# A fused attention and feed-forward layer on one core: first unit's attention moved beside the last-but-two projection, last output tile split in two column halves

## The reference

```python
def reference(x, w_qkv, b_qkv, w_out, b_out, gate_w, up_w, down_w, gate_s, up_s, down_s):
    h = layernorm(x)
    q, k, v = split(h @ w_qkv.T + b_qkv)              # 16 heads of 32
    # linear attention with decay, chunks of 128 tokens:
    #   out = (q * decay_q) @ S + ((q @ k.T) * dmask) @ v
    #   S   = lam_c * S + (k * decay_k).T @ v
    x = x + layernorm(attention(q, k, v) @ w_out.T + b_out)
    h = layernorm(x)
    g = silu((h @ fp8(gate_w)) * gate_s) * ((h @ fp8(up_w)) * up_s)
    return x + layernorm((g @ fp8(down_w)) * down_s)
```

## Time and profile before

| | us |
|---|---|
| median of 3 runs | 980.73 |
| profiled execution | 980.54 |
| its span, first to last instruction | 978.7 |
| TensorE busy | 949.6 (97%) |
| VectorE busy | 696.8 (71%) |
| GpSimd busy | 691.3 (71%) |
| ScalarE busy | 510.6 (52%) |
| mean granted clock of TensorE | 0.997 |

### The profile page before, as it was taken

The page is one execution under the profiler, slowest core; times in us unless marked ns, Lnnn a source line. Parts: engine busy times, 40 slices in busy tenths (PEclk is TensorE's granted clock), DMA queues, the critical chain, the costliest instruction groups (busy, mean ns, idle before and its releaser), DMA issues.

```text
span 978.7 us, 21882 instructions
## 1 busy us (share of the span) xinstructions
PE 949.6 (97%) x8412; PEld 700.8 (72%) x8412; DVE 696.8 (71%) x1357; ACT 510.6 (52%) x987; POOL 691.3 (71%) x839
## 2 busy tenths in 40 slices
PE   8999999999888999999999999999999999999996
PEld 7687777777666776867778776767767676776764
DVE  6999998985887775767567576766757676675422
ACT  5666555565655464636355463635546363544522
POOL 3799998887776585948567584856758495775633
PEclk9999999999999999999999999999999999999998
DMA  9798899989976673846658284665838475512100
GB/s 320 232 309 245 244 261 314 281 260 301 244 204 144 138 195 66 183 108 142 157 103 190 55 199 97 152 146 115 180 59 199 94 161 121 139 44 44 44 23 22
DMA packets 199354, 159.87 MB, mean 163 GB/s; under 512 B 141649, under 2 KB 141777, under 8 KB 199121
## 3 DMA queue, kind: packets, MB, share of 16 engines
q1 hardware_dynamic: 198384, 157.86, 65.3%
q10 hardware_dynamic: 864, 0.61, 0.2%
HBM read 82.93 MB, written 41.94 MB: 128 GB/s over the span
## 4 chain that ended last, share of the span: by engine, by line
PE 44%; DVE 18%; POOL 16%; issue 10%; DMA 4%; SPq 3%; ACT 3%; POOLq 0%; DVEq 0%; ACTq 0%
PE bank L919 18%; PE bank L937 17%; PE att L896 5%; DVE stats L1386 3%; POOL rstd L1053 3%; POOL att_pool L1118 3%; DMA dram_qk<-qk_hl 2%; POOL vv L1103 2%; DVE state_hl L1460 2%; POOL qk_hl L1083 2%; SPq L297 2%; DVE w_pool L1523 2%; POOL xr L1128 1%; POOL rstd L1050 1%; DVE state L1449 1%
## 5 line engine op out<-in xcount | busy, mean ns | idle before, releaser
L919 PE MATMUL bank<-f_pool,up_q 128*128 128x256 f16 x1536 | 183.7, 273 | 4.2 <-DVE w_pool L1523 2.8
L919 PE MATMUL bank<-f_pool,gate_q 128*128 128x256 f16 x1536 | 183.6, 273 | 4.1 <-ACT w_pool L617 3.9
L937 PE MATMUL bank<-down_q,w_pool 128*128 128x512 f16 x768 | 168.3, 379 | 0.0
L919 PEld LDWEIGHTS bank<-f_pool,up_q 128*128 128x128 f16 x1536 | 148.1, 98 | 26.8 <-DVE w_pool L1523 8.5
L919 PEld LDWEIGHTS bank<-f_pool,gate_q 128*128 128x128 f16 x1536 | 146.3, 98 | 26.9 <-ACT w_pool L617 6.5
L1118 POOL TENSOR_TENSOR att_pool<-p,att_pool 128x512 f16<-128x512 f32 x128 | 145.7, 1159 | 24.5 <-ACT att_pool L569 24.5
L1523 DVE SCALAR_TENSOR_TENSOR w_pool<-bank,us_t,w_pool 128x256 f32<-128x256 f32 x192 | 84.1, 480 | 109.9 <-ACT w_pool L617 54.7
L1050 POOL TENSOR_TENSOR rstd<-mv,eps_t 128x1 f32<-128x1 f32 (+1 forms) x113 | 32.4, 287 | 182.0 <-DVE mv L1392 181.8
L937 PEld LDWEIGHTS bank<-down_q,w_pool 128*128 128x128 f16 x768 | 74.1, 98 | 86.9
L1136 POOL TENSOR_TENSOR w_pool<-w_pool 128x512 f16<-128x512 f32 x96 | 111.2, 1164 | 29.3 <-ACT w_pool L623 29.2
L569 ACT CAST att_pool<-p 128x512 f16<-128x512 f32 x128 | 75.6, 619 | 53.7 <-DVE p L1430 53.0
(11 more groups left out here) (147 smaller groups left out, 1824.4 us busy)
## 6 DMA issues: line engine op xcount, KB each, us to landing
dram_qk<-qk_hl SPq DMA_DIRECT2D x64, 256.0 KB, 4.6
att_pool<-dram_qk SPq DMA_DIRECT2D x64, 256.0 KB, 6.0
f_pool<-dram_qk SPq DMA_DIRECT2D x64, 256.0 KB, 6.0
xr<-in_x SPq DMA_DIRECT2D x31, 512.0 KB, 4.6
dram_kd<-kd_hl SPq DMA_DIRECT2D x32, 256.0 KB, 2.8
dram_v<-vv SPq DMA_DIRECT2D x32, 256.0 KB, 4.4
qn_pool<-dram_qk SPq DMA_DIRECT2D x32, 256.0 KB, 9.1
out_x<-w_pool SPq DMA_DIRECT2D x32, 256.0 KB, 2.1
```

The source lines that it names most:

```text
L919: ins = nc.tensor.matmul(b[:, j * TOK:(j + 1) * TOK], w[:, k, o * P:(o + 1) * P], x1_hl[:, v % 2, part, k], start=(k == 0 and part == 0), ...
L937: ins = nc.tensor.matmul((b_gate, b_up)[t][:, :], h_hl[:, part, k, t * P:(t + 1) * P], down_q[:, k], start=(k == 0 and part == 0), stop=(k ...
```

## The change

- A new `last_ahead` replaces `ahead(13)` on TensorE, ScalarE, GpSimd and VectorE. It has the scores of unit 0's first chunk between qk(13,2) and v(13,0), and the state of that chunk between the v blocks. The v blocks of unit 13 go to `b_gate` and `b_up`, as `b_s` now holds scores.
- `first_slot` attends chunk 0 after qk(14,0), then works on chunk 1, whose `attend(0, 1)` and the first scores of unit 1 stand ahead of v(14,1).
- `second_slot` has qk(15,0) and qk(15,1) apart, both project blocks together, and qk(15,2) and qk(15,3) behind attend(1,0). The orders of ScalarE, GpSimd and VectorE change with it.
- On SP, spill_v(13) goes ahead of load_xr(0); turn_o_tile(0,0) and spill_kd(14) move up.
- In slot 17, y2_normalise(14, 0) stands behind silu(15, 0).
- Tile 1 of unit 15 is made in two halves of 256 columns in two banks (48 matmuls of 256 columns), scaled and summed by halves, centred on VectorE while GpSimd takes the root, finished by VectorE, and stored by two DMAs, one from ScalarE's queue and one from SP's.

```diff
         def v_bank(n, t):
-            return b_s[t][:, :] if n < LEAD else (b_gate, b_up)[t][:, :]
+            return b_s[t][:, :] if n < LEAD - 1 else (b_gate, b_up)[t][:, :]
...
+            spill_v(LEAD - 1)
             load_xr(0)
-            spill_v(LEAD - 1)
             spill_q(LEAD)
+            turn_o_tile(0, 0)
             sp.wait_ge(score_mm, 8)
             load_unit(2, 0)
             load_unit(2, 1)
-            turn_o_tile(0, 0)
             spill_k(LEAD)
             sp.wait_ge(state_mm, 2)
             load_unit(2, 3)
+            spill_kd(LEAD)
             turn_o_tile(0, 1)
-
-            spill_kd(LEAD)
             spill_v(LEAD)
...
-            store(units - 1, 1)
...
+            sp.wait_ge(last_d, 2)
+            sp.dma_start(last_tile[:, cols(1)], y2[:, 1, cols(1)]).then_inc(stored[1], 16)
...
             def second_slot():          # ScalarE
                 n = LEAD + 1
+                o_hi_tile(0, 1)
+                probs_hi(1, 0, 0)
                 q_hi(n, 0)
-                o_hi_tile(0, 1)
+                v_hi_tile(LEAD, 1)
+                probs_hi(1, 0, 1)
                 q_hi(n, 1)
-                probs_hi(1, 0, 0)
                 state_hi(1, 0)
                 y_normalise(0, 0)
-                probs_hi(1, 0, 1)
+                y_normalise(0, 1)
+                probs_hi(1, 1, 0)
+                x1_hi(0, 0)
                 k_hi(n, 2)
-                y_normalise(0, 1)
-                k_hi(n, 3)
-                x1_hi(0, 0)
-                probs_hi(1, 1, 0)
                 x1_hi(0, 1)
                 probs_hi(1, 1, 1)
                 state_hi(1, 1)
+                k_hi(n, 3)
...
                 silu(v, 0)
+                if v == units - 1:
+                    y2_normalise(v - 1, 0)
...
-                y2_normalise(v, 0)
-
+                if v != units - 2:
+                    y2_normalise(v, 0)
...
+            act.wait_ge(last_d, 1)
+            act.dma_start(last_tile[:, cols(0)], y2[:, 1, cols(0)]).then_inc(stored[1], 16)
...
+            def down_by_halves(v):
+                pe.wait_ge(h_d, 6 * v + 6)
+                for h, b in enumerate((b_up, b_gate)):
+                    if h:
+                        pe.wait_ge(y2_d, 2 * v + 1)
+                    for k in range(IT):
+                        for part in range(2):
+                            ins = nc.tensor.matmul(b[:, cols(h)], h_hl[:, part, k, P:TOK], down_q[:, k, cols(h)],
+                                                   start=(k == 0 and part == 0), stop=(k == IT - 1 and part == 1))
+                    ins.then_inc(down_mm, 1)
...
+            def last_ahead():           # TensorE
+                k = LEAD - 1
+                for i in range(3):
+                    project_qk(k, i)
+                scores(0, 0, 0)
+                project_qk(k, 3)
+                scores(0, 0, 1)
+                project_v(k, 0)
+                carry_and_state(0, 0)
+                project_v(k, 1)
+
             def first_slot():
-                scores(0, 0, 0)
-                carry_and_state(0, 0)
                 project_qk(LEAD, 0)
-                scores(0, 0, 1)
-                project_qk(LEAD, 1)
-                project_qk(LEAD, 2)
                 attend(0, 0)
                 scores(0, 1, 0)
+                project_qk(LEAD, 1)
+                scores(0, 1, 1)
+                carry_and_state(0, 1)
+                project_qk(LEAD, 2)
                 project_qk(LEAD, 3)
-                scores(0, 1, 1)
                 project_v(LEAD, 0)
-                carry_and_state(0, 1)
+                attend(0, 1)
+                scores(1, 0, 0)
                 project_v(LEAD, 1)
-                attend(0, 1)
 
             def second_slot():
                 n = LEAD + 1
-                scores(1, 0, 0)
                 project_qk(n, 0)
+                scores(1, 0, 1)
                 project_qk(n, 1)
                 carry_and_state(1, 0)
                 project(0, 0)
-                scores(1, 0, 1)
                 project(0, 1)
-                project_qk(n, 2)
-                project_qk(n, 3)
                 attend(1, 0)
                 scores(1, 1, 0)
-                project_v(n, 0)
+                project_qk(n, 2)
                 scores(1, 1, 1)
                 carry_and_state(1, 1)
+                project_qk(n, 3)
+                project_v(n, 0)
                 project_v(n, 1)
                 attend(1, 1)
...
+            def last_ahead():           # GpSimd
+                k = LEAD - 1
+                inverse_std_x(k + 2)
+                v_lo(k - 1)
+                state_decay(0, 0)
+                q_lo(k, 0)
+                q_lo(k, 1)
+                probs_lo(0, 0, 0)
+                x_lo(k + 2)
+                kd_lo_half(k, 0)
+                probs_lo(0, 0, 1)
+                kd_lo_half(k, 1)
+
             def first_slot():
-                state_decay(0, 0)
-                probs_lo(0, 0, 0)
-                probs_lo(0, 0, 1)
                 v_lo(LEAD - 1)
+                state_decay(0, 1)
                 q_lo(LEAD, 0)
+                probs_lo(0, 1, 0)
                 q_lo(LEAD, 1)
-                state_decay(0, 1)
-                probs_lo(0, 1, 0)
+                probs_lo(0, 1, 1)
                 kd_lo_half(LEAD, 0)
-                probs_lo(0, 1, 1)
                 kd_lo_half(LEAD, 1)
-                v_lo(LEAD)
 
             def second_slot():
                 n = LEAD + 1
                 state_decay(1, 0)
+                probs_lo(1, 0, 0)
+                v_lo(LEAD)
                 q_lo(n, 0)
-                probs_lo(1, 0, 0)
+                probs_lo(1, 0, 1)
+                inverse_std_of(LN_Y, 0, 0)
+                inverse_std_of(LN_Y, 0, 1)
+                residual(0, 0)
                 q_lo(n, 1)
-                inverse_std_of(LN_Y, 0, 0)
-                residual(0, 0)
-                probs_lo_block(1, 0, 2)
-                inverse_std_of(LN_Y, 0, 1)
-                probs_lo_block(1, 0, 3)
                 residual(0, 1)
                 inverse_std_of(LN_X1, 0, 0)
-                state_decay(1, 1)
+                probs_lo(1, 1, 0)
                 inverse_std_of(LN_X1, 0, 1)
                 x1_lo(0, 0)
-                probs_lo(1, 1, 0)
                 x1_lo(0, 1)
+                state_decay(1, 1)
                 probs_lo(1, 1, 1)
...
+            def last_part(h):
+                dve.wait_ge(down_mm, 2 * units + h)
+                nc.vector.tensor_tensor(y2[:, 1, cols(h)], (b_up, b_gate)[h][:, cols(h)], ds_t[:, cols(h)], ALU.mult).then_inc(y2_d, 1)
+                dve.wait_ge(y2_d, 2 * units + h)
+                nc.vector.bn_stats(stats[:, LN_Y, h], y2[:, 1, cols(h)]).then_inc(bn_d[LN_Y2], 1)
...
+            def last_ahead():           # VectorE
+                k = LEAD - 1
+                moments_x(k + 2)
+                scale_h()
+                k_lo(k, 2)
+                dve.wait_ge(tab_in, 16 * N_TAB)
+                dve.wait_ge(*x_landed(units - 2))
+                masked(0, 0, 0)
+                k_lo(k, 3)
+                masked(0, 0, 1)
+                v_sum(k, 0)
+                carry_and_state(0, 0)
+                v_sum(k, 1)
```

More of the change, by code:

```diff
@@ L257, in over_e, with cols @@
             return table.unsqueeze(2).to_broadcast([P, KT, DH])
+        last_tile = out_u[units - 1, T - 1]
+        def cols(h):
+            return slice(h * D // 2, (h + 1) * D // 2)
         def third(w, part, half):
@@ L1021, in slot @@
                 else:
-                    for t in range(T):
-                        down(v, t, 0, IT)
+                    down(v, 0, 0, IT)
+                    down_by_halves(v)
             pe.wait_ge(eps_d, 3)
@@ L1039, in _ @@
             project_first(3)
-            for k in range(LEAD):
+            for k in range(LEAD - 1):
                 ahead(k)
+            last_ahead()
             first_slot()
@@ L1570, in ahead, with last_ahead @@
                     v_sum(k, t)
-            for k in range(LEAD):
+            for k in range(LEAD - 1):
                 ahead(k)
-            dve.wait_ge(tab_in, 16 * N_TAB)
-            dve.wait_ge(*x_landed(units - 2))
+            def last_ahead():
+                k = LEAD - 1
+                moments_x(k + 2)
[9 more added lines that the diff above has]
+                v_sum(k, 1)
             def first_slot():
-                masked(0, 0, 0)
-                carry_and_state(0, 0)
-                masked(0, 0, 1)
                 state_lo(0, 0)
-                k_lo(LEAD, 2)
                 masked(0, 1, 0)
                 out_sum(0, 0)
-                k_lo(LEAD, 3)
                 masked(0, 1, 1)
@@ L1588, in first_slot @@
                 scale_o(0, slice(0, 1), 1)
+                carry_and_state(0, 1)
+                o_lo_tile(0, 0)
+                k_lo(LEAD, 2)
+                state_lo(0, 1)
+                k_lo(LEAD, 3)
                 v_sum(LEAD, 0)
-                o_lo_tile(0, 0)
-                carry_and_state(0, 1)
```

(10 more changed lines are left out.)

88 lines of the change are left out of this document (60 added, 28 removed).

## The result

The changed kernel takes 986.95 us (median of 6 runs, 983.68 to 989.85) where the kernel before takes 981.19 in the same comparison (6 runs, 979.71 to 984.08). The ratio is 1.0054, with a 95% interval from 1.0038 to 1.0070: slower by half a per cent. I had forecast 980.8 and a range up to 983.3.

The account below looks back on a forecast made before the run. It took TensorE's idle time, mostly where the stages meet (236.99 to 297.34 us), to bound the kernel. 980.54 - 2.1 + 3.9 - 0.7 + 2.2 - 0.95 - 2.1 = 980.8 us, range 977.3 to 983.3.

Parts of the forecast that it names:

- part 1: From 221.34 us to the end of project(0,1): pauses of 3.35 instead of 5.4 us, a gain of 2.1.
- Part 2: From project(0,1) to gate_up(0,0): pauses of 8.8 instead of 4.9 us, 5.0 before v(15,1), a loss of 3.9.
- Part 3: Behind the pause before v(15,1): the granted clock falls to 1.2 GHz, costing 2.2 us (0 to 5.3).
- rival A: The forecast itself: pause before v(15,1) and fall of the clock, 980.8 us; chance 0.47.
- rival B: The clock holds through the pause before v(15,1), 978.6 us; chance 0.21.
- what slot 2 gives back: After gate_up(0,0): silu, which made TensorE wait, is now in time; 0.7 us taken back (0 to 1.3).
- Parts 4 and 5: Last slot's start: silu ahead of y2_normalise(14,0), gain 0.95 us; tail: halves of 256 columns, gain 2.1.
- Rival E: Tail: the halves do not shorten the end, as the narrower store lands later; 982.9 us, chance 0.05.
- C: First stretch runs without its two pauses, project(0,1) over 3.35 us earlier; 977.4 us, chance 0.15.
- D: The clock stays at 1.2 GHz from v(15,1) until gate_up(0,0), costing 5.3 us; 983.9 us, chance 0.12.

Follow-up runs that it names:

- e5: Changed kernel with spill_kd(14) and turn_o_tile(0,1) ahead of all loads of unit 2 on SP: 981.07 us, ratio 0.9999.
- e10: Changed kernel with the old second-slot order on the four compute engines, its own SP order kept: 980.98 us, ratio 0.9996.
- e8: e5 with the old second-slot order on the four compute engines: 974.96 us, ratio 0.9938.
- e9: e5 with only state_decay(1,1) on GpSimd moved ahead of unit 0's norms: 980.65 us, ratio 0.9998.
- e6: e5 with matmuls of constants in the two pauses before the v blocks of unit 15: 979.10 us, ratio 0.9977.
- e1: Kernel before with only the last tile in column halves, stored on two queues, and y2_normalise(14,0) behind silu(15,0): 979.42 us, ratio 0.9972.
- e3: Changed kernel with matmuls of constants in the two pauses before the v blocks of unit 15: 985.08 us, ratio 1.0029.
- e4: Changed kernel with the turned tile ahead of unit 2's keys, the decay ahead of unit 0's norms, unit 15's k_hi, k_lo earlier: 978.67 us, ratio 0.9967.
- e7: e5 with the decay ahead of unit 0's norms and unit 15's k_hi, k_lo ahead of its second norm: 976.58 us, ratio 0.9954.

## Why the prediction was wrong

**One step failed, and it was worth 3.4 us in the traces and 5.4 by the ratios.** It is the end of part 1, which put the wait for the turned tile at nothing: "turn_o(0,1) follows the load of unit 2's keys and is needed at 271.6; I have it landing at 270". It was needed at 272.25 and landed at 272.27 + 3.5 = 275.8. I had moved SP's instructions along with the waits ahead of them and kept each one's own time, and so took 4.94 us for the keys' load. But the keys landed 16.8 us after the first stack before and 17.3 after. Since the loads of unit 2 started 1.25 us later, the keys ended later too, though they were issued 3.3 us earlier. The rows of before held the warning: the tile was issued at 269.96, landed at 273.06 (3.1 us later), and project(0,1) began at 273.67, with 0.6 us to spare. Counted from qk(13,0), the new order wants it 1.9 us earlier, so 1.3 us of waiting were certain unless the tile moved up; it came 2.3 us later instead. The change's spill_kd(14) ahead of the tile (271.18 to 272.27) adds 1.1 of that. The same mistake stands in the prediction's turn_x(15), there with the other sign: its two transposes were issued 3.5 us later and held SP for 5.29 us, not 8.06, so that what stands behind them moved by 0.7 us and not by 3:

```profile
240.71 5.29 SPq L304 DMA_TRANSPOSE xr<-hl  x2
```

e5 takes the failed step away and lands on the forecast: 981.07 against 980.8, and ratio 0.9999. The price follows twice, as 1.0054 less 0.9999 (5.4 us) and as e10 less e8 (5.7), each known to about 2 us each way. In the traces project(0,1) is over 53.2 us after qk(13,0) in e5 and 56.64 in the change, a difference of 3.4. The rest of the 5.4 may be the clock at the tile's pause or chance.

**The rest of part 1 was right.** Pauses of 0.89 + 0.20 before scores(0,0,1) (forecast 1.4) and 1.91 before v(14,0) (1.9). Without the wait for the tile, project(0,1) would have been over at 274.4 on the scale of before (forecast 274.2). Alone, in e8, it gains 1.9.

**Part 2 was right, link by link.** The chain behind v(15,1), from GpSimd, VectorE and ScalarE of the changed kernel, answering to the earlier trace rows:

```profile
280.44 0.19 POOL L1093 TENSOR_TENSOR rstd<-mv,eps_t 128x1 f32<-128x1 f32 x1 [5.02 <-DVE mv L1453]
...
292.46 0.40 POOL L1154 TENSOR_TENSOR state_d<-state,lam 128x128 f32<-128x128 f32 x1
...
292.95 1.19 DVE L1510 TENSOR_TENSOR state<-bank,state_d 32x128 f32<-32x128 f32 x4 [0.84 <-issue]
...
294.17 1.26 ACT L588 ACTIVATE state_hl<-state 32x128 f16<-32x128 f32 x4 [1.87 <-DVE state L1510]
295.46 0.84 ACT L547 ACTIVATE qk_hl<-bank,bqk 128x256 f16<-128x256 f32 x2
...
296.33 0.88 DVE L1470 SCALAR_TENSOR_TENSOR kd<-bank,bqk,decay_k 128x256 f32<-128x256 f32 x2 [2.19 <-ACT qk_hl L547]
```

GpSimd's run of steps from the root of tile (0,1) to the decay took 12.4 us (280.44 to 292.86), as worked out. The pauses were 0.94, 2.31 and 3.22 where I had 1.0, 2.5 and 5.0; the last is shorter because v(15,0) ran at the low clock and took 1.69 us more, which lies inside the wait: 3.22 + 1.69 = 4.9. e9 corrects the reading, though: with the decay out of that chain v(15,1) came only about 1 us sooner, since the state's sum also stood behind k_lo(15,2), and so behind the same layer norm on ScalarE. (The 5.3 us that the prediction puts "behind v(15,1)" contain v(15,1) itself; measured, with its low clock taken off, they are 5.25.)

**Part 3 was right in kind, and in size by luck.** The clock fell, as rival A had it and rival B had not, and the price, which I had chosen at 2.2 us without a row to carry it, is 2.0 by e5 and e6. It also fell one block earlier than forecast: v(15,0) lost 1.69 us behind a pause of 2.31, which stayed without effect only because v(15,1) had to wait anyway. In the profiled run of the change the price is 1.54 us of v(15,1); parts 2 and 3 together are 5.3 there against a forecast of 6.1, and 6.0 by e5 and e8, where the forecast, with what slot 2 gives back, comes to 5.4. The place was drawn too narrowly. I wrote that the pauses of 1.7 and 1.8 before had left the clock alone. In other executions it fell behind pauses of 1.79 (e1) and 1.68 (e1 and e8) and at the tile's pause (e3, e4, e10). The Trainium skill, "TensorE: Matmul & The Clock Gate", section "HAM oscillation — how this bites in real kernels", tells of a kernel in which each wait for a transfer put the next block of work at the low level. The trace of e10 agrees (4.25 us for 2.76), and the profiled run of the change does not: its project(0,1) took 2.76 behind 3.44 us of waiting.

**Parts 4 and 5 were right.** The timelines at the end and at the start of the last slot, answering to the earlier trace rows:

```profile
946.94 0.84 ACT L624 ACTIVATE w_pool<-bank,gs_t 128x256 f32<-128x256 f32 x2 [10.75 <-PE bank L942]
...
976.57 0.42 DVE L1598 TENSOR_TENSOR w_pool<-bank,ds_t 128x256 f32<-128x256 f32 x1 [1.64 <-PE bank L973]
...
978.05 0.60 POOL L1187 TENSOR_TENSOR rstd<-rstd,eps_t 128x1 f32<-128x1 f32 x1
...
978.76 0.88 DVE L1611 SCALAR_TENSOR_TENSOR w_pool<-w_pool,rstd,xr 128x256 f32<-128x256 f32 x2 [0.51 <-POOL rstd L1187]
...
979.66 0.33 SPq L490 DMA_DIRECT2D out_x<-w_pool  x1
```

The last matmul ends at about 976.53 (0.04 ahead of the scaling, as in the earlier trace rows), the store is issued 3.1 us later (forecast 3.05, before 5.16) and the end comes 2.2 us behind it (before 2.5): a gain of 2.27 against 2.1. silu starts with the last slot, without the normalisation ahead of it, and the gap of 0.94 is gone. Rival E is refuted by e1. Slot 2 gave back 0.75 (forecast 0.7), the later ones 0.4 more.

**The rivals** C and D did not happen: the pauses of part 1 came, and the clock was back before gate_up(0,0). None of the five held the mechanism that decided. I had allowed for a late transfer with turn_x(15), at 0 "and at up to 2 if it lands later", and gave none to turn_o(0,1), which had the least reserve of all.

**What stays open.** The changed kernel's median lies 3.3 us above its profiled run, and the mean clocks of its other runs are lower (0.991 to 0.994 against 0.996). A fall of the clock at the tile's pause, as e3, e4 and e10 show it, would account for about 1.5 us of that in each such run. The start of the kernel is another candidate, which I had not weighed: in the twelve profiled runs qk(13,0) starts anywhere from 220.98 (e5) to 225.42 (e1), though no edit touches the order of the work ahead of it, and in e1 and e4, the two latest, the granted clock of 15 to 30 us was 0.82 and 0.89 where the other ten show 1.00. I have no trace of a slower run of the change itself, so neither share is placed. In e7 the time from gate_up(0,0) to the end is 1.7 us longer than in e8 (678.7 and 677.0), and nearly all of it lies in slot 2 (45.8 and 44.2 us up to gate_up(1,0)); I have not followed it further.

## What to carry to other kernels

When SP's order is changed, do not move a transfer's issue with its old duration: take the start of the batch of loads and the time that the whole batch needed to land, and see which small transfer stands behind it and by how much it was in time before. That time is a better guess than the instruction's own, for a small shift; moved by 11 us, as in e5, it changed as well (17.3 to 14.2). A small transfer that TensorE waits for belongs ahead of the loads that nobody wants yet; here three moved lines were worth 5.4 us by the ratios and turned a loss of 0.5% into no change, and with the old second slot into a gain of 0.6%. And where engines alternate between the steps of two stages, what the next matmul waits for (here k_hi and k_lo) goes ahead of the layer norm that has slack: 4.5 us between e5 and e7 (with the early decay, which alone won nothing that could be measured in e9).
